# Feed-forward phases that send each token's rows only to its two experts, through device memory, instead of running every expert over every token

## The reference: what is computed

```
x = x + 0.5 * ffn(layernorm(x))
x = x + attention(layernorm(x))
x = x + 0.5 * ffn(layernorm(x))

def ffn(x):                                   # x: 8192 x 128, E = 8 experts, D = 128, F = 256
    scores = x @ router                       # 8192 x 8
    top 2 experts of each row; gates = sigmoid(score) for those two, 0 for the other six
    xe  = x * gate[e]                         # for each expert e
    out = sum over e of (silu(xe @ w_in[e]) * (xe @ w_gate[e])) @ w_out[e]
    return out + (silu(x @ w_in_s) * (x @ w_gate_s)) @ w_out_s      # the shared expert
```

## Time and profile before

| | |
|---|---|
| median of 3 runs | 2944.68 us (2943.84 to 2947.04) |
| the profiled execution: own time, span | 2947.33 us, 2945.5 us |
| first feed-forward phase, from its first unit on PE | 31.5 us to 754 us |
| attention | 754 us to about 2214 us |
| second feed-forward phase, from its first unit on PE | 2223.9 us to the end |
| mean granted clock of PE | 0.961 |

### The profile page before, as it was taken

The page is one execution under the profiler, slowest core; times in us unless marked ns, Lnnn a source line. Parts: engine busy times, 40 slices in busy tenths (PEclk is TensorE's granted clock), DMA queues, the critical chain, the costliest instruction groups (busy, mean ns, idle before and its releaser), DMA issues. The chain is left out here.

```text
span 2945.5 us, 60238 instructions
## 1 busy us (share of the span) xinstructions
PE 2752.1 (93%) x18624; PEld 1985.9 (67%) x18624; DVE 1893.1 (64%) x4781; ACT 1735.6 (59%) x3222; POOL 1392.2 (47%) x1728
## 2 busy tenths in 40 slices
PE   5999999999499999999999999999998999999999
PEld 4777777777255666566666565666656777777777
DVE  7666666667256666666666666666647666666665
ACT  4656566655256666556666555666646656665655
POOL 3555555555444344444434444444414555555554
PEclk9999999999689999999999999999998999999999
DMA  4000000000377788888878877887831000000000
GB/s 115 1 0 0 0 0 0 0 0 1 66 220 221 223 235 230 213 219 224 226 219 224 225 213 215 229 224 228 230 103 50 8 7 4 7 7 4 7 6 9
DMA packets 233801, 324.94 MB, mean 110 GB/s; under 512 B 29444, under 2 KB 188548, under 8 KB 233604
## 3 DMA queue, kind: packets, MB, share of 16 engines
q1 hardware_dynamic: 194436, 171.36, 24.5%
q0 software_dynamic: 36864, 150.49, 15.3%
q10 hardware_dynamic: 2304, 0.61, 0.1%
HBM read 141.68 MB, written 154.92 MB: 101 GB/s over the span
## 5 line engine op out<-in xcount | busy, mean ns | idle before, releaser
L1089 DVE CUSTOM_DVE_ANT_0 at_junk<-at_ps_s,at_rel 128x512 bf16<-128x512 f32 x1024 | 666.1, 688 | 403.9 <-PE at_ps_s L758 386.3
L895 ACT ACTIVATE at_probs<-at_ps_t 128x512 f32<-128x512 f32 x1024 | 558.7, 595 | 504.5 <-PE at_ps_t L743 504.3
L378 POOL TENSOR_TENSOR ffn_h_lo<-ffn_h,ffn_h_hi 128x512 fp32r<-128x512 f32 x384 | 502.1, 1311 | 475.6 <-ACT ffn_h_hi L305 475.6
L489 DVE TENSOR_TENSOR ffn_h<-ffn_silu,ffn_ps_gate 128x512 f32<-128x512 f32 x576 | 393.7, 683 | 406.7 <-ACT ffn_silu L348 404.4
L305 ACT CAST ffn_h_hi<-ffn_h 128x512 fp32r<-128x512 f32 x576 | 358.8, 623 | 408.4 <-DVE ffn_h L489 407.0
L194 PE MATMUL ffn_ps_mid<-ffn_xT_hi,ffn_w_mid 128*128 128x512 f32 x1152 | 480.2, 417 | 22.7 <-DVE ffn_h L489 11.5
L743 PE MATMUL at_ps_t<-tab_ident,at_rel 128*128 128x128 f32 x3328 | 497.1, 290 | 0.0
L194 PE MATMUL ffn_ps_gate<-ffn_xT_hi,ffn_w_gate 128*128 128x512 f32 x1152 | 456.7, 396 | 0.0
L194 PE MATMUL ffn_ps_out<-ffn_h_hi,ffn_w_out 128*128 128x512 f32 x1152 | 453.9, 395 | 0.2
L743 PEld LDWEIGHTS at_ps_t<-tab_ident,at_rel 128*128 128x128 f32 x3328 | 372.2, 146 | 82.3 <-issue 22.7
L348 ACT ACTIVATE ffn_silu<-ffn_ps_mid 128x512 f32<-128x512 f32 x576 | 343.8, 597 | 80.2 <-PE ffn_ps_gate L194 73.2
(11 more groups left out here) (161 smaller groups left out, 4000.2 us busy)
## 6 DMA issues: line engine op xcount, KB each, us to landing
at_band<-at_src POOLq DMA_DIRECT2D x256, 574.0 KB, 4.8
at_rel<-at_band SPq DMA_DIRECT2D x512, 143.5 KB, 3.8
at_qs<-at_q_hi SPq DMA_DIRECT2D x128, 64.0 KB
at_ks<-at_k_hi SPq DMA_DIRECT2D x128, 64.0 KB
at_rel<-at_band SPq DMA_DIRECT2D x64, 128.0 KB, 3.5
at_rel<-at_band SPq DMA_DIRECT2D x64, 127.5 KB, 3.1
at_rel<-at_band SPq DMA_DIRECT2D x64, 112.0 KB, 2.9
at_rel<-at_band SPq DMA_DIRECT2D x64, 111.5 KB, 3.5
```

The lines of the kernel that those rows point to most:

```text
L378: pool.tensor_tensor(h_lo[:, u % RH, :], h[:, u % RH, :], h_hi[:, u % RH, :].bitcast(F32), ALU.subtract).then_inc(hlo_pool.sem, 1)
L489: dve.tensor_tensor(h[:, u % RH, :], silu[:, u % RH, :], ps_gate[:, u % 2, :], ALU.mult).then_inc(h_done.sem, 1)
L895: act.activation(probs[:, kp, 2 * hp + i].rearrange("p n q -> p (n q)"), ps_t[:, i, :], ACT.Exp).then_inc(exp_done.sem, 1)
L1089: dve.tensor_tensor_reduce(out=junk[:, i, :], in0=ps_s[:, i, :], in1=rel[:, c % RREL, l, h, :], scale=1.0, scalar=-3e38, op0=ALU.add, op1= ...
```

## The change

`ffn_phase` is written anew; attention is untouched. The order of work in a phase is now:

1. 16 jobs "A", one for each tile of 512 tokens: normalise, transpose, split, score with the router, run the **shared** expert (2 units, with weights in `w_shared`), and add its result to `X` (`add_shared`). DVE chooses two experts for each row, for two tiles at a time (`choose`), PE counts rows by expert (`rank`), and DVE turns the counts into a row number for each token and choice (`number`). ACT scales the rows by both gates (`scale`, 8 instructions a tile). POOL sends them to device memory, sorted by expert (`scatter`: 8 indirect DMAs a tile, each of 128 rows of 512 bytes).
2. 46 jobs "B", each a dense tile of 512 rows of one expert. A group of 10 token tiles makes 27 jobs, the second group, of 6 tiles, makes 19 (2 x tiles + 7, so that every split of rows over experts fits). SP reads the expert's number and the place of the rows from SBUF, loads 768 KB of split weights (`w_expert`, 4 buffers) and 256 KB of rows (`xg`, 3 buffers) from device memory, and stores each result of 256 KB (`rows_out`, `store_rows`).
3. POOL fetches two result rows for each token (`gather`: 8 indirect DMAs a tile), and DVE adds them to `X` (`add_routed`). Tiles 0 to 7 are added during the second group's jobs, at every second job, tiles 8 to 15 after the last job (`LATE`).

All of `h_low` is on DVE now, and POOL does only DMAs. `ps_out` holds one job (2 units), so `leave`, `turn_out` and the way out of PSUM come once every 2 units instead of once every 18. `output` runs 3 units behind (`LAG`). Both phases are written out without a hardware loop. In the first phase SP also clears 14 pieces of the row buffer (`zero`, 256 KB each) ahead of the shared weights, and stores the split weights to device memory.

The core of the diff, shortened (new names: `n` a job, `c` its half, `u` = 2n + c a unit, `m` an earlier job):

```diff
+        LAG = 3
+        RN, RG, RW, RX, RZ = 6, 3, 4, len(rows.sent), len(rows.z_in)      # RX = 2, RZ = 3
 # SP
+            def load_expert(n):
+                if m == 0:
+                    sp.wait_ge(map_done, 2 * (g + 1))
+                    for e in range(E):
+                        at = sp.value_load(filled_i[0:1, g, e:e + 1], ...)
+                        sp.dma_start(rows.x[g][bass.ds(at, W)]..., zero[:]).then_inc(cleared, 16)
...
+                which_e = sp.value_load(which_i[0:1, g, m:m + 1], min_val=0, max_val=E)
+                if b_of(n) >= RW:
+                    sp.wait_ge(out_done, 2 * (n - RW) + 2)
+                sp.dma_start(w_expert[:, n % RW].bitcast(F32), rows.w[bass.ds(which_e, 1)]...)
+                at = sp.value_load(where_i[0:1, g, m:m + 1], ...)
+                sp.dma_start(xg[:, n % RG], rows.x[g][bass.ds(at, W)]...)
...
+            for n in range(NA - 2, JOBS + 4):
+                if NA <= n + 2 < JOBS:
+                    load_expert(n + 2)
+                if NA <= n - 4 < JOBS:
+                    store_rows(n - 4)
 # PE
+            def output(u):
+                n, c = divmod(u, C)
+                pe.wait_ge(hhi_done, u + 1)
+                pe.wait_ge(hlo_done, u + 1)
+                if c == 0 and n > 0:
+                    pe.wait_ge(oT_done, n)
...
+            for n in range(JOBS + 3):
+                for c in range(C):
+                    u = 2 * n + c
+                    if c == 0 and is_a(n):
+                        score(n)
+                    if n < JOBS:
+                        unit(n, c)
+                    if c == 0 and n + 1 < JOBS:
+                        turn_in(n + 1)
+                    if 0 <= u - LAG < C * JOBS:
+                        output(u - LAG)
+                    if c == 0 and 0 <= n - 3 < JOBS:
+                        turn_out(n - 3)
+                    if c == 1 and n % 2 == 0 and 2 <= n <= NA:
+                        rank((n - 2) // 2)
 # ACT
+            for n in range(JOBS + 4):
+                for c in range(C):
...
+                    if n < JOBS:
+                        act.wait_ge(mid_done, u + 1)
+                        act.activation(silu[:, u % RH, :], ps_mid[:, u % 2, :], ACT.Silu)
+                    if 0 <= u - 1 < C * JOBS:
+                        h_high(u - 1)
+                    if c == 0 and n + 1 < JOBS:
+                        x_high(n + 1)
+                    if c == 1 and 0 <= n - 2 < JOBS:
+                        leave(n - 2)
+                    if c == 0 and 0 <= n - 2 < NA:
+                        scale(n - 2)                 # waits for the scatter of tile n - 4
 # POOL
+            def scatter(t):
+                pool.wait_ge(scaled, t + 1)
+                pool.wait_ge(index_done, q + 1)
+                for k in range(2):
+                    for s in range(T):
+                        pool.indirect_dma_start(rows.x[g], bass.IndirectOffsetOnAxis(index[...], 0), xe[...], None)
+            for t in range(NA):
+                scatter(t)
+            for g, (lo, hi) in enumerate(GROUPS):
+                last = FIRST_B[g] + TILES[g] - 1
+                for n in (last - 1, last):
+                    pool.wait_ge(z_out[n % 2], 16 * (b_of(n) // 2 + 1))
+                for t in range(lo, hi):
+                    gather(t)                        # 8 indirect DMAs, waits for z_added of tile t - 3
 # DVE
+            for t in LATE:                           # tiles 8 to 15
+                add_routed(t)
```

More of the change, by code:

```diff
@@ L25, in wait, with clear, _ @@
         eng.wait_ge(self.sem, n * self.per + c)
+class Buffers:
+    pass
+def clear(nc, signals):
+    numbers = [s.num for s in signals]
+    low, high = min(numbers), max(numbers) + 1
+    assert len(set(numbers)) == high - low
+    with nc.Block() as block:
+        @block.gpsimd
+        def _(pool):
+            pool.sem_clear(range(low, high))
 def mean_and_variance(dve, STATS, work, done):
@@ L107, in ffn_phase @@
[L107 to L121, removed]
@@ new lines, in ffn_phase, with weight_of, pieces_at, gathered_at @@
+        z_in = rows.z_in
+        z_step, z_added, stored = signal("z_step"), signal("z_added"), rows.stored
+        block = phase.enter_context(nc.Block())
+        def weight_of(n, part, c):
+            piece = (lambda x: w_shared[:, x, :]) if is_a(n) else (lambda x: w_expert[:, n % RW, x, :])
+            return lambda a: piece(2 * part + a)[:, c * P:(c + 1) * P]
+        def pieces_at(n):
+            return [i for i in (2 * n - 2, 2 * n - 1) if first and 0 <= i < PIECES]
+        def gathered_at(n):
+            t = (n - FIRST_B[1] - 3) // 2
+            return t if n < JOBS and (n - FIRST_B[1] - 3) % 2 == 0 and GROUPS[0][0] <= t < GROUPS[0][1] else None
@@ new lines, in _ @@
+            for n in range(NA - 2, JOBS + 4):
[3 more added lines that the diff above has]
+                    store_rows(n - 4)
+                if store is not None and gathered_at(n - 1) is not None:
+                    store_result(gathered_at(n - 1))
+            if store is not None:
+                for t in LATE:
+                    store_result(t)
+                sp.wait_ge(stored, 16 * NA)
+            if first:
+                sp.wait_ge(shared_in, 16)
@@ new lines, in unit @@
+            def unit(n, c):
+                u = 2 * n + c
+                if c == 0:
+                    pe.wait_ge(xlo_done, n + 1)
+                    if n == 0:
+                        if first:
+                            pe.wait_ge(raw_lo, 3)
+                        else:
+                            pe.wait_ge(shared_in, 16)
+                    elif not is_a(n):
+                        pe.wait_ge(weights_in[n % RW], 16 * (b_of(n) // RW + 1))
+                if u >= 2:
+                    pe.wait_ge(h_done, u - 1)
+                for part, dst in ((0, ps_mid), (1, ps_gate)):
+                    ins = product(dst[:, u % 2, :], weight_of(n, part, c), lambda b: (xT_hi, xT_lo)[b][:, n % 2, :], True, True)
+                ins.then_inc(mid_done, 1)
@@ new lines, in leave @@
+            def leave(m):
+                act.wait_ge(out_done, 2 * m + 2)
+                if m > 0:
+                    act.wait_ge(out_turned, m)
+                act.copy(oT[:], ps_out[:]).then_inc(oT_done, 1)
+            def weight_high(i):
+                k = i % RAW
+                part = i % 3
+                to = w_shared[:, 2 * part, :] if i < 3 else w_expert[:, (i // 3 - 1) % RW, 2 * part, :]
+                act.wait_ge(raw_in[k], 16 * (i // RAW + 1))
+                if i >= 3 and i // 3 - 1 >= RW:
+                    act.wait_ge(kept, 16 * (i // 3 - 1 - RW + 1))
+                act.activation(to, raw[:, k, :], ACT.Copy, scale=0.5 if part == 2 else 1.0).then_inc(raw_hi, 1)
@@ L530, in attention_phase @@
+            for t in LATE:
+                add_routed(t)
+        phase.close()
+        if first:
+            clear(nc, signals)
 def attention_phase(nc, io, X, STATS, tables):
```

897 lines of the change are left out of this document (511 added, 386 removed).

## The result

The changed kernel took 2977.39 us (median of 4 runs, 2972.57 to 2983.67), the kernel before 2944.26 beside it: ratio 1.0114, 95% interval 1.0097 to 1.0131. It is slower by 1.1%; the forecast was 2720 us, 7.6% faster, with a range up to 2930. But a later sitting on another chip gave 2761.04 us for the same instructions, ratio 0.9374 (0.9336 to 0.9411), while the medians of the kernel before stay between 2940 and 2950 on every chip.

What follows compares the result with a forecast made beforehand. PE's instruction count was taken to bound the feed-forward phases. Phase one 647.5 us (-106), phase two 600 (-122), attention unchanged: span 2945.5 - 228 = 2717.5, time 2720 us, range 2610 to 2930.

Steps and rivals of the forecast that it cites:

- The step that failed: POOL's scatters in jobs A: 8.8 us a tile at 1.1 each, hidden under the job's 11.4 us up to 1.42 each.
- my rivals: Clock falls in jobs B (0.25), indirect DMAs bound it (0.12), transfers bind (0.07), wait for the copy not paid (0.06).
- the three signs: POOL as releaser under ACT's xe in jobs A; PE waiting for w_expert or xg; PEclk under 0.9 in B jobs.
- An indirect DMA: POOL's gathers and scatters: 1.1 us each, chosen between 0.71 (direct DMA's row) and twice that, 1.42.
- the page's time, 3025: Whole kernel: about 3025 us if POOL stood still for the skill page's 2.15 us per indirect DMA of 64 KB.
- Jobs A: 16 shared-expert jobs a phase: 9.8 us each plus 1.6 for the clock, 11.4 each, 182 us.
- the clock term: Jobs A: PE's clock drops after waits, costing up to 3.4 us a job; half taken, 1.6 us.
- Jobs B: 46 expert jobs a phase: 5.08 us of PE work plus 2.17 waiting for the copy, 7.25 each, 333.5 us.
- the clock falls in jobs B: Rival: PE's clock falls after each job's 2.17 us wait, 1.7 us more a job, 2876 us; chance 0.25.
- Start of group two: DVE waits 12 us for group one's first gather; SP's eight clears hold up loads and stores about 5 us.
- Tail: End of each phase: last store 3.3, 48 bare gathers 52.8, landing 2.2, last additions 2.7: 61 us; draining the pipeline 6.
- What the copy's wait is worth: Jobs B: ACT's copy oT behind the second silu and split makes PE wait 2.17 us a job, 269 us in all.

Runs made afterwards that it cites:

- The best version: v2_all with SP issuing the load of a job's rows ahead of its expert's weights: 2715.29 us on chip 2, 2686.25 and 2703.15 on chip 8.
- v2_all: Changed kernel with copy oT ahead of the second silu, scatters meant in rows of 4, group one's gathers paced and added two jobs later: 2712.31 us, ratio 0.9235.

## Why the prediction was wrong, point by point

**The step that failed** is "Scatter: 8 x 1.1 = 8.8 us a tile, under the 11.4 of a job A (...), so hidden up to 1.42 each", and the same for the gathers of group one. I costed an indirect DMA by POOL's time alone. POOL's time was nearly right and the scatters did lie under the jobs A. But on three of the six later chips, and on that of the result, PE's signals come late beside them, and the phases are longer by 104 and 110 us than on a chip on time. None of my rivals was this, and none of the three signs by which I'd have called the prediction wrong came up: ACT's `xe` waits for DVE's gates and not for POOL, what PE waits for `xg` in the steady jobs B is at most 0.4 us at a time, and the clock there is 1.00. The range ended 47 us short. The groups of POOL's indirect DMAs and, of ACT's timeline, the scaling of one tile, on the slower chip:

```profile
L496 POOL DMA_INDIRECT rows_x<-ffn_xe,rows_index x256 | 251.0, 980 | 381.8 <-DVE rows_index L598 304.7 <-issue 77.0
L506 POOL DMA_INDIRECT ffn_zg<-rows_z,rows_home x256 | 247.3, 966 | 631.4 <-issue 504.4 <-DVE X L673 105.7 <-DMA rows_z<-ffn_y 21.4
...
166.15 2.44 ACT L450 ACTIVATE ffn_xe<-ffn_xn,ffn_gate 128x128 f32<-128x128 f32 x8 [1.44 <-DVE ffn_gate L579]
```

The other terms can be read on the chip on time, where nothing else disturbs them:

- **An indirect DMA**, forecast 1.1 us: 0.97 busy and 0.30 of issue, 1.26 from start to start in a row. The Trainium skill, "DMA: Bandwidth & Descriptors", section "Anatomy of one DMA", gives an estimate of 2.15 for POOL, if it stood still for the whole of such a DMA. It does not: the trace has 1.26. As the time from issue to landing, which is what the page says most of it is, the figure agrees: the median here is 2.2 us. That the page's time, 3025, is nearer to 2977 is chance; the mechanism is another.
- **Start**: first unit at 47.1 us, forecast 46.
- **Jobs A**: 47.1 to 231.7 us for 16, 11.5 each, forecast 11.4. Part of that agreement is luck: the first three take 6.5 to 6.9 and 14.9 us, the later ones mostly by turns some 10.5 and 13, which the forecast did not have. ACT's eight pieces take 2.44 us (last row above), forecast 2.4. PEclk 0.78 there: the clock term was right in kind.
- **Jobs B**: 7.08 us steady, forecast 7.25, with PE's wait for the copy 1.77 us (2.17), clock 0.98 to 1.00. The rival "the clock falls in jobs B" did not come. In group two, beside the gathers, a job takes 7.5.
- **Start of group two**: 10.1 us more than a job (5), wait of DVE for the first `zg` 14.9 (12).
- **Tail**: the 48 bare gathers take 65.4 us (607.5 to 672.9), forecast 61; drain and last job 18.6 for 13.
- **Sums**: phase one 672.9 us, forecast 647.5; phase two, from its first unit, 620 for 600. Attention is 8 us shorter than before (1446 for 1454, within the spread of all runs), forecast 0. The time on that chip, 2761, lies 1.5% over the forecast and inside the range.
- **What the copy's wait is worth**: I priced it at 269 us of loss. Taking it away gave 28 to 38, most of it in the jobs A, as in the jobs B the load of the rows, queued on SP behind a load that waits for an output, was next. Only both together gave PE alone as the pace: 5.06 us a job, forecast 5.08.

## What to carry to other kernels

Cost a DMA from POOL not only by POOL's own time: look at whether other engines' waits end late beside it, and where a kernel leans on indirect DMAs, measure it on several chips before believing one number, above all when the one beside it (the kernel before, without them) stays the same. Replace indirect DMAs by direct ones wherever the place is known, and keep rows of them short (4 in a row by themselves cost nothing beside jobs B; 8 and 4 with 0.8 us between cost as much as 12). A wait that is to break up a row does so only if it isn't fulfilled yet when the engine comes to it: count the rows in the trace of the new version before reading its time as that of short rows. On a queue that runs in order, put the load that waits for nothing ahead of the one that waits, and when a wait is removed, name the next before pricing the gain.

## What was unexpected of the hardware

- On chips 14, 2 and 8 (and that of the result) PE's signals reach DVE, ACT and POOL late beside indirect DMAs: extra rows cost 4.7 us in all behind 8 in a row, 9.6 behind 16, 19.5 behind 24, and one silu came 22.8 late behind 32. In the two traces of the changed kernel there, 36 of 248 silus are over 1 us late; on chips 9, 5 and 1 no version has one. DVE gets ACT's signals within 0.1 us on both kinds, and direct DMAs of POOL (24 in a row, 12.6 us) do nothing.
- An indirect DMA of 128 rows of 512 bytes can be issued every 1.26 us, a direct one every 0.53.
- Open: what in the chip holds the signals, whether a chip is always of one kind (chip 8 was in both of its sittings, the others had one each), and what of the indirect form does it. How long a row lasts is not it alone (12.6 us of direct ones nothing, 10.1 us of indirect ones 4.7); but an indirect DMA also keeps POOL busy about twice as long as a direct one, and reads or writes rows in no order, and these were not parted.
- The best version beats the kernel before on both chips it met, of the late kind: 2686 to 2715 us against 2944 to 2949 beside it. The changed kernel did not run beside it; on two other late chips it took 2977 and 2982. On a chip on time it was not run; v2_all took 2712 there.
